# A two-layer graph attention and transformer block: work around the stage barrier and inside the attention slots moved

## What is computed

```python
def layer0(v, q, adj):            # v [8,512,512], q [8,512]; self features and masks
    self_feat = concat(v, q) @ W_self.T + b_self
    for d in range(2):            # two directions, 20 keys, 16 heads
        out += gat_attention(self_feat, ...)      # masked softmax over 20 keys
    return v + relu(out)

def layer1(hidden, w):            # hidden [8,512,512], 16 heads of 32
    h = sln(hidden, w)            # layer norm, scaled and shifted by rows from w
    q, k, v = split(h @ Wqkv.T + bqkv)
    att = softmax(q @ k.T) / sqrt(512)
    h1 = (att @ v) @ Wp.T + bp + hidden
    return sln(h1, w) + h1
```

## Time and profile before

| quantity | value |
|---|---|
| median of 3 runs | 1351.17 us (1349.26 to 1354.97) |
| profiled execution | 1355.45 us, its span 1353.6 us |
| TensorE busy | 1248.8 us (92%) |
| VectorE busy | 891.5 us (66%) |
| GpSimd busy | 882.3 us (65%) |
| ScalarE busy | 615.2 us (45%) |
| attention, first score matmul to last | 501.9 to 1323.8 us |
| VectorE maxima (L1635) | 496 of 674 ns |
| ScalarE exponentials (L1526) | 512 of 597 ns |
| GpSimd sums of 1024 columns (L1356, L1361) | 180 of 2.39 us |

### The profile page before, as it was taken

One profiled execution on the slowest core, in us unless ns is written; L12 is line 12 of the kernel. 1 busy time (PEld: TensorE's weight loads), 2 busy tenths in 40 slices (PEclk: granted clock), 3 DMA queues, 4 the chain that ended last, 5 costly groups with the idle time before them and its releaser, 6 DMA issues.

```text
span 1353.6 us, 20343 instructions
## 1 busy us (share of the span) xinstructions
PE 1248.8 (92%) x6100; PEld 831.7 (61%) x6100; DVE 891.5 (66%) x1448; ACT 615.2 (45%) x1076; POOL 882.3 (65%) x565
## 2 busy tenths in 40 slices
PE   7879899999999788899999999999999999999983
PEld 4347677777777666466656666666565566566551
DVE  3445578778778754756766776776675776676745
ACT  1322252445244434454454464464464455455452
POOL 1114467676776734765795796795796696696733
PEclk9979899999999888899999999999999999999987
DMA  9663254445444653433543442542442542542410
GB/s 340 253 224 110 63 191 172 157 158 222 159 155 146 202 192 89 126 86 72 149 110 71 135 124 67 142 123 65 139 127 56 144 116 69 145 116 69 115 47 32
DMA packets 104454, 178.60 MB, mean 132 GB/s; under 512 B 38832, under 2 KB 48368, under 8 KB 99104
## 3 DMA queue, kind: packets, MB, share of 16 engines
q1 hardware_dynamic: 92816, 145.22, 35.3%
q10 hardware_dynamic: 11536, 32.14, 7.9%
HBM read 81.04 MB, written 45.38 MB: 93 GB/s over the span
## 4 chain that ended last, share of the span: by engine, by line
PE 29%; DVE 12%; POOL 9%; issue 6%; DMA 3%; ACT 3%; SPq 1%; ACTq 0%; DVEq 0%; POOLq 0%
PE a_bank L1808 6%; PE a_bank L1759 6%; DVE rden L1653 5%; POOL acc L1361 4%; PE a_bank L1772 4%; PE a_bank L106 4%; DVE keep L1635 4%; PE a_bank L107 4%; PE a_bank L108 4%; PE a_bank L1819 2%; DMA out_y<-h 1%; ACT pt L1526 1%; POOL acc L1356 1%; DMA h<-h_rows 1%; DVE rden L1661 1%
## 5 line engine op out<-in xcount | busy, mean ns | idle before, releaser
L1635 DVE TENSOR_REDUCE keep<-a_bank 128x1 f32<-128x512 f32 x496 | 331.5, 674 | 256.5 <-PE a_bank L1772 254.1
L1526 ACT ACTIVATE pt<-a_bank 128x512 f32<-128x512 f32 x512 | 300.5, 597 | 376.5 <-PE a_bank L1759 322.9
L1361 POOL TENSOR_TENSOR acc<-acc,pt 128x1024 f32<-128x1024 f32 x120 | 286.5, 2387 | 32.4 <-ACT pt L1526 25.2
L1759 PE MATMUL a_bank<-sq_stack,sk_stack 98*128 98x512 f32 x512 | 221.7, 433 | 19.6 <-ACT pt L1526 7.5
L1772 PE MATMUL a_bank<-sk_stack,sq_stack 96*128 96x512 f32 x496 | 209.4, 422 | 4.5 <-DVE keep L1635 4.4
L1356 POOL TENSOR_TENSOR acc<-pt 128x1024 f32<-128x1024 f32 x60 | 143.6, 2393 | 77.4 <-PE a_bank L1819 65.4
L1759 PEld LDWEIGHTS a_bank<-sq_stack,sk_stack 98*128 98x128 f32 x512 | 98.0, 191 | 115.5 <-issue 71.7
L1065 PE MATMUL g_bank<-m,sf 128*128 128x320 f32 x512 | 147.5, 432 | 0.8 <-issue 0.8
L1653 DVE RECIPROCAL rden<-a_bank 128x128 f32<-128x128 f32 x128 | 120.6, 944 | 17.9 <-PE a_bank L1802 17.9
L1772 PEld LDWEIGHTS a_bank<-sk_stack,sq_stack 96*128 96x128 f32 x496 | 95.9, 193 | 48.6 <-DVE keep L1635 33.0
L1808 PE MATMUL a_bank<-pt,v 128*32 128x512 f32 x1024 | 124.7, 605 | 0.0
(11 more groups left out here) (200 smaller groups left out, 2496.0 us busy)
## 6 DMA issues: line engine op xcount, KB each, us to landing
sq_stack<-qh SPq DMA_DIRECT2D x256, 64.0 KB, 2.0
sk_stack<-kh SPq DMA_DIRECT2D x256, 64.0 KB, 2.1
m<-m_rows SPq DMA_DIRECT2D x8, 1280.0 KB, 6.7
xraw<-in_x_t SPq DMA_DIRECT2D x8, 1024.0 KB, 8.8
xn<-in_x SPq DMA_DIRECT2D x8, 1024.0 KB, 5.2
h_rows<-xn ACTq DMA_DIRECT2D x8, 1024.0 KB, 4.8
t_rows<-houth SPq DMA_DIRECT2D x8, 1024.0 KB, 3.9
t_rows<-houtl SPq DMA_DIRECT2D x8, 1024.0 KB, 6.5
```

The lines of the kernel that those rows point to most:

```text
L1361: nc.gpsimd.tensor_tensor(acc[:, two, :], acc[:, two, :], pt[:, step + 1, two, :], ALU.add).then_inc(s["sum_done"], 1)
L1526: nc.scalar.activation(pt[:, i, 2 * half + k, :], bank[:, k, :], ACT.Exp).then_inc(s["exp_done"], 1)
L1635: nc.vector.reduce_max(mx[:, half, k, n:n + 1], bank[:, 2 + e % 2, :], AX).then_inc(s["emax_done"], 1)
L1759: nc.tensor.matmul(bank[:, k, :], sk[c % 2][0:3 * DH + 2, j, i * P:(i + 1) * P], sq[c % 2][0:3 * DH + 2, j, :], start=True, stop=True).the ...
```

## The change

No computation is added or removed. In `graph`: in the last step GpSimd does its four scalings without `add_bp` between them and the four additions after them; VectorE scales a bias column later; SyncE issues the stacks of chunk 1, half 1, before the barrier and leaves the store of batch 7's rows to the next block. In `attention`: SyncE issues that store right behind the load of the output weights; the store of tile 0 stands between the copies of q and of k, those of tiles 2 and 3 and the row load come later. GpSimd does result 1 ahead of an `rsqrt`, result 2 at the start of chunk 3, result 3 at its end. ScalarE takes `project` of q in slot 3, the result copies in slot 10, `normalise` of tiles 2 and 3 later, `load_h` of tiles 0 and 1 in chunk 0 of the next batch and of tile 2 in slot 13, and the second part of `load_t` in slot 14. VectorE takes the low part of q in slot 3, the reciprocals in slots 4, 5, 7 and 8, the quotients in slot 9 and the low part of k in slot 10.

```diff
--- before.py
+++ after.py
@@ -467,7 +467,7 @@
         assert nc.sbuf_base == at["out"]
-        houth, houtl = sb("houth", [P, FC, N], F32R), sb("houtl", [P, FC, N], F32R)
+        houth, houtl = t["houth"], t["houtl"] = sb("houth", [P, FC, N], F32R), sb("houtl", [P, FC, N], F32R)
         assert nc.sbuf_base == at["acc"]
@@ -634,10 +634,11 @@
             stacks(1, 0)
+            stacks(1, 1)
             sp.wait_ge(la["sh_lo"], 1)
...
                          sht[:, 1, :].bitcast(F32)).then_inc(la["shrow_lo"], 16)
-            store_t(B - 1, 4 * B)
+            sp.wait_ge(s["hl_done"], 4 * B)
 
@@ -657,7 +658,7 @@
 
-            def softmax(b, has_former):
+            def softmax(b, has_former, last=False):
                 for i in range(NT + 2):
@@ -670,8 +671,11 @@
                         nc.gpsimd.tensor_tensor(v, v, keys(rc[:, i - 2]), ALU.mult).then_inc(s["w_done"], 1)
-                        if has_former:
+                        if has_former and not last:
                             add_bp(b - 1, i - 2)
+                if last:
+                    for i in range(NT):
+                        add_bp(b - 1, i)
 
@@ -707,7 +711,7 @@
                     lo_rows(b - 2)
-                softmax(b, True)
+                softmax(b, True, last)
 
@@ -1005,8 +1009,6 @@
 
-            dve.wait_ge(la["ld_c"], 16)
-            nc.vector.tensor_scalar(bcol3[:, 2, :], bcol3[:, 2, :], float(D) ** -0.5, None, ALU.mult).then_inc(la["bv_done"], 1)
             nonzero_rows(0)
@@ -1014,6 +1016,8 @@
             steps(dve, step)
+            dve.wait_ge(la["ld_c"], 16)
+            nc.vector.tensor_scalar(bcol3[:, 2, :], bcol3[:, 2, :], float(D) ** -0.5, None, ALU.mult).then_inc(la["bv_done"], 1)
             lo_part(0, 0)
@@ -1274,15 +1278,17 @@
         def _(sp):
-            def stacks(b, c, half):
+            def stacks(b, c, half, which=(0, 1)):
 
...
                     sp.wait_ge(s["et_ready"], SLOTS * (G - 2) + 8 * half + 8)
-                for ready, src, dst, at, done in (
-                        (s["qh_done"], qh, sq, (0, 2 * DH), stq), (s["ql_done"], ql, sq, (DH,), stq),
-                        (s["kh_done"], kh, sk, (0, DH), stk), (s["kl_done"], kl, sk, (2 * DH,), stk)):
+                for n, ready, src, dst, at, done in (
+                        (0, s["qh_done"], qh, sq, (0, 2 * DH), stq), (0, s["ql_done"], ql, sq, (DH,), stq),
+                        (1, s["kh_done"], kh, sk, (0, DH), stk), (1, s["kl_done"], kl, sk, (2 * DH,), stk)):
+                    if n not in which:
+                        continue
                     sp.wait_ge(ready, need)
@@ -1311,26 +1317,32 @@
                     later = not first(b)
-                    if c < 3 or more:
+                    if (c < 3 or more) and not start(b, c):
                         stacks(*ahead(b, c, 1), 1)
...
                     if c == 3 and later:
-                        store_y(b - 1, 3)
-                    if c == 3:
-                        load_rows(b)
+                        store_y(b - 1, 2)
+                    if c == 0 and not first(b) and not (isinstance(b, int) and b == 1):
+                        store_y(b - 2, 3)
+                    if c == 0 and later:
+                        load_rows(b - 1)
                     if c < 2 or more:
-                        stacks(*ahead(b, c, 2), 0)
+                        stacks(*ahead(b, c, 2), 0, (0,))
+                    if c == 1 and later:
+                        store_y(b - 1, 0)
+                    if c < 2 or more:
+                        stacks(*ahead(b, c, 2), 0, (1,))
                     if c < 3 or more:
                         shift_lo(*ahead(b, c, 1), 0)
-                    if c == 1 and later:
-                        store_y(b - 1, 0)
-                    if c == 2 and later:
-                        store_y(b - 1, 2)
 
             sp.dma_start(t["wp_raw"][:, :, :], d["wp_t"].rearrange("(c p) o -> p c o", p=P)).then_inc(w_in[3], 16)
+            for k, src in enumerate((t["houth"], t["houtl"])):
+                sp.dma_start(d["t_rows"][B - 1, k], src[:, :, :].bitcast(F32)).then_inc(t["t_stored"], 16)
             batches(sp, batch)
+            store_y(B - 2, 3)
+            load_rows(B - 1)
             for i, (y, _) in enumerate(last_tiles()):
@@ -1392,14 +1404,14 @@
                         key_sum(*(ahead(b, c, -1) if c else (b - 1, 3)), 1, 2)
+                    if later and c > 1:
+                        result(b - 1, c - 1)
                     if later and c in (1, 2):
                         rsqrt(b - 1, 2 * c - 2)
-                    if later and c in (2, 3):
-                        result(b - 1, 2 * c - 3)
                     if not final(b, c):
                         key_sum(b, c, 0, 0)
-                    if later and c in (1, 2):
-                        result(b - 1, 2 * c - 2)
+                    if later and c == 1:
+                        result(b - 1, 0)
                     if first(b) and c in (1, 2):
@@ -1421,6 +1433,8 @@
                         output_lo(b, 1)
+                    if later and c == 3:
+                        result(b - 1, 3)
 
@@ -1560,33 +1574,35 @@
                             values(b + 1, 1 - bpar, 0, KB)
-                        if slot == 2 and c in (2, 3) and later:
-                            normalise(b - 1, 2 * c - 3)
+                        if slot == 2 and c == 2 and later:
+                            normalise(b - 1, 1)
+                        if slot == 4 and c == 3 and later:
+                            normalise(b - 1, 3)
                         if slot == 2:
                             shift_hi(b, c, 1)
-                        if slot == 4 and (c < 2 or more):
+                        if slot == 3 and (c < 2 or more):
                             project(*ahead(b, c, 2), 0)
-                        if slot == 5 and c in (1, 2) and later:
+                        if slot == 4 + c and c in (1, 2) and later:
                             normalise(b - 1, 2 * c - 2)
...
                         if later:
-                            if slot == 15 and c == 1:
+                            if slot == 13 and c == 1:
                                 load_h(b - 1, 2)
...
                                 load_h(b - 1, 3)
-                        if slot == 1 and c == 3 and more:
-                            load_h(b, 0)
-                        if slot == 10 and c == 3 and more:
-                            load_h(b, 1)
+                        if slot == 6 and c == 0 and later:
+                            load_h(b - 1, 0)
+                        if slot == 8 and c == 0 and later:
+                            load_h(b - 1, 1)
                         if slot == 11:
...
                                 shift_hi(*ahead(b, c, 1), 0)
-                        if slot == 11 and c == 1 and more:
+                        if slot == 14 and c == 1 and more:
                             load_t(b + 1, (1,))
-                        if slot == 9:
+                        if slot == 10:
                             if c == 0 and later:
@@ -1703,17 +1719,17 @@
                                 variance(b - 1, 2 * c - 1)
-                        if slot == 5 and (c < 2 or more):
-                            lo_part(*ahead(b, c, 2), 0)
                         if slot == 3:
                             shift_lo(b, c, 1)
-                        if 4 <= slot < 8 and former:
-                            reciprocals(*former, slot - 4)
-                        if slot == 8 and former:
+                            if c < 2 or more:
+                                lo_part(*ahead(b, c, 2), 0)
+                        if slot in (4, 5, 7, 8) and former:
+                            reciprocals(*former, slot - 4 - slot // 6)
+                        if slot == 9 and former:
                             quotients(*former)
...
                             shift_lo(*ahead(b, c, 1), 0)
-                        if slot == 9 and (c < 2 or more):
+                        if slot == 10 and (c < 2 or more):
                             lo_part(*ahead(b, c, 2), 1)
```

## The result

The changed kernel takes 1336.15 us, the median of six runs (1324.51 to 1343.4), against 1353.3 for the kernel before on the same chips (1349.26 to 1357.35): a ratio of 0.986, with a 95% interval of 0.981 to 0.991. The change gains 17 us; 42 were forecast, and the time is 2 us above the upper end of the range. Its runs spread over 19 us, those of the kernel before over 8.

A forecast was written before the change was run, and what follows sets the result against it. TensorE was taken to bind, so only its gaps or slow matmuls could go. Gains of 30.3 + 6.5 + 2.3 + 2.0 - 2.4 + 3.6 = 42.3 us, off the median 1351.17, gave 1309 us; range 1297 to 1334.

The forecast's parts named there:

- stores and loads around chunk 1: Chunks 1 and 2: earlier store and load remove a 3.0 us loss, 1.2 left for late transfers; gain 1.8 a batch.
- graph's end: Before the barrier: four bias additions in a row on GpSimd end later, a loss of 2.4 us (1.5 to 3.5).
- the loop's edges: Batches 1 to 6: the window's 5 us beyond six times batch 3, of which half was kept.
- Spread reciprocals: VectorE, chunks 0 and 3: spreading its work stops TensorE's waits in slots 8 to 10; gain 1.2 us in both together.
- B: Rival: ScalarE's chain after the quotients binds, so spreading VectorE's work frees nothing; 1321 us, chance 0.13.
- GpSimd's results: Chunk 3, slot 3: reordered results bring chunk 2's last key sum earlier, so the denominators' stall goes; gain 1.6 us.
- the shift row: End of chunk 1: starts 0.6 us later, goes out 4 us ahead of use, needing as little as 3.67; fits narrowly.
- Rival A: Handover from chunk 1 to 2 becomes the new wait: 3.0 us instead of 1.2 in seven batches, 1322 us, chance 0.15.
- T: Experiments' rival theory, around chunk 1's end: DMA traffic is the limit, so any order of transfers leaves a wait somewhere.
- First chunk: Batch 0 after the barrier: stack copies issued before it remove ScalarE's 5.47 us wait; 23.2 us, 6.5 less.
- Rival E: Half 1's row lands after all moved stores, 6 us for 0.7, and splits hold GpSimd, 3 more: 1317 us, chance 0.04.
- Last batch: Chunks 0 and 1 gain 1.1 us, chunk 2 gains 3.5, chunk 3 loses 1.0 on result 2's low part; net 3.6.

The follow-up runs named there:

- e5: e2 with reciprocals back in slots 4 to 7, quotients in 8, low parts of q and k and ScalarE's copies as before: 1325.27 us, ratio 0.982.
- e6: e2 with the order of GpSimd's results and ScalarE's normalisation of tile 3 as in the kernel before: 1324.64 us, ratio 0.981.
- e2: Changed kernel with the load of tile 2's rows moved from slot 13 to 15, behind the second half in slot 14: 1312.53 us, ratio 0.971.
- e4: e2 with tile 0's store back behind the k copies and the shift row: 1323.41 us, ratio 0.980.
- e13: e1 with the load of tile 2's rows in slot 15 instead of 13: 1331.01 us, ratio 0.986.
- e14: e13 with tile 0's store back behind the k copies and the shift row: 1328.15 us, ratio 0.983.
- e9: e2 with the barrier as before: last rows' stores ahead of it, stack copies of chunk 1's second half behind it: 1315.61 us, ratio 0.976.
- e7: e2 with the bias additions of the graph's last batch back between GpSimd's scalings: 1313.29 us, ratio 0.972.
- e8: e2 with ScalarE's two copies of result 2 back in slot 9, in the last chunk only: 1314.14 us, ratio 0.972.
- e3: Kernel before with the second half of the next batch's rows in slot 14 of chunk 1 instead of 11: 1340.84 us, ratio 0.994.
- e1: Changed kernel with the second half of the next batch's rows back in slot 11 of chunk 1: 1329.09 us, ratio 0.985.
- e10: e1 with the second half moving a quarter of its columns, 256 KB instead of 1 MB, so computing something else: 1307.70 us, ratio 0.968.

## Why the prediction was wrong

The failed step is one term of the sum, the gain of 1.8 us a batch from the stores and loads around chunk 1; a smaller one, the graph's end, was off too and hidden by luck. All terms, against spans of the profiled executions:

| step | forecast | found |
|---|---|---|
| chunks 0 and 3, batches 1 to 6 | 16.8 | 18.2 |
| chunks 1 and 2, batches 1 to 6 | 10.8 (and 2.7 at the loop's edges) | -9.3 |
| batch 0 | 8.8 | 8.7 |
| graph's end and barrier | -0.4 | -2.3 |
| from the program's start to the graph's first bias addition, nothing changed | 0 | 2.1 |
| last batch up to its last slot | 3.6 | 0.6 |
| sum | 42.3 | 18.0 |

The 2.7 at the loop's edges weren't there: batch 3, from which the steady part was taken (102.0), was the second shortest of the six in the kernel before, whose mean is 102.9; most of the difference lies in chunk 1 of batch 2 (27.1) and chunk 3 of batch 4 (28.9).

- **Spread reciprocals.** Right: the earlier trace rows's surplus goes, slots 8 and 9 of chunk 0 take 1.16 to 1.18, and 0.2 to 0.3 a chunk is left behind ScalarE's result copies, of which I had left 0.3. e5 confirms it, and B was wrong.
- **GpSimd's results.** Right, 1.6 by e6; result 3 at the end of chunk 3 costs nothing.
- **Stores and loads around chunk 1.** The failed step. Its direction was named, "a wait of TensorE in slot 2 of chunk 2", and its arithmetic had the half 0.6 late. Two inputs were too small. The last issue was put 2.1 behind the start of slot 14 and came 2.9 behind it (849.14, slot 14 beginning at 846.23), because the load ahead of it waited for a store issued only 5.6 us earlier. And the landing was taken as the 5.8 of the earlier trace rows and was 7.4. The sum has the half at 856.5 instead of 854.1, against the 853.5 that I had as the need (TensorE was there at 853.7). From there on every us of lateness counts in full, so a surplus of 0.6 became 2.84; and I had booked no price for the slot behind a wait, in which the clock falls: 8.0 of the 30.4 us. The other half of the term, the shift row, was right: chunk 1 hands over without a wait in all six batches. The row goes out 3.5 to 3.8 us ahead of its use, as the narrow margin said, and completes in 2.5 to 3.5, since the second half now comes behind it; the 3.67 of the earlier trace rows was too much here.
- **Rival A** had the place and the sign, with 15% of the chances and a price of 3.0 a batch, copied from what the kernel before lost there. Nothing bounded it by that: the batch lost 5.1 there (30.4 in six). It should have been priced from the lateness, with "5.2 available, 5.8 needed" as the sign of a cliff, and its end put into the range.
- **What T adds.** Even a timely half is not free. It, its first half, the twelve copies and the store share the DMA engines, so in slot 11 it delays the k copies and the row, and in slot 14 it is itself late. I had treated the landing times as fixed and the edits as independent; e2, e4, e13 and e14 show that they are neither.
- **First chunk.** 23.05 against 23.2, in part by luck. The sum had 1.4 for the lower clock and 0.7 for the row; the row cost nothing and the lower clock 2.1 in slots 0 and 1, since slot 1 now ran at it throughout (2.19 us at a granted clock of 0.50, 1.65 at 0.70 before). Rival E had the order right and the price wrong: the stores were issued by 502.2 and the last took 10.2 us, to 511.9; the row, issued at 509.43, completed at 512.2, behind them, but slot 8 needs it only at 513.7. What the Trainium skill (DMA: Bandwidth & Descriptors, Queues, rings and completion order) says of ring order fits that row, without being shown by it.
- **Graph's end.** The wait is 2.9 us longer than in the kernel before and 3.3 longer than in e7, where I took 2.4 with an end of 3.5. The barrier opens 1.2 us sooner by e9 (41.5 us from ScalarE's copy to the first score matmul, 40.3 in e2), not 2.0. From the graph's first bias addition to the first score matmul the changed kernel takes 325.25 us and the kernel before 322.96. That attention began only 0.2 later was luck: the stretch ahead of that addition, the same code in both, took 176.91 instead of 178.96 (176.0 to 179.3 in the sixteen executions). Beside VectorE's weight splits three of the four additions take 1.71 and the first 1.27, and the four splits 6.75 together, 1.74 each, where one without an addition beside it takes 0.68 (e7). By the rule of the Trainium skill (SBUF — State Buffer, Who interferes with whom) each addition would have been held for a pass. The trace agrees that the two engines hold each other up, but not on the size: an addition beside a split loses 0.44, less than the 0.68 of a pass, and the first loses nothing.
- **Last batch.** Chunk 2 gained 3.1 (3.5 forecast). Chunk 3 lost 3.7 instead of 1.0: the low part was 1.56 later in slot 11, and the low clock behind the longer wait made slots 12 to 14 longer by 2.2. e8 takes both away (2.72, 0.93, 0.94 and 4.60).

Slots 0 to 3 of chunk 2 in e2 still take 0.6 us more a batch than without loss, and slot 15 ahead of them 0.9. The 0.9 is the wait for the row, which takes 3.9 to 5.8 us there; of the 0.6 most is batch 4, where slots 0 to 2 take 6.6 instead of 3.6 behind that wait. Why the row took 5.8 in batch 4 (slot 15 at 3.65) and 4.0 in batch 3 (1.76), issued 0.2 us behind the first load of the second half both times, stays open.

## What to carry to other kernels

When a load is moved behind an instruction that waits for another DMA, its time is that DMA's landing plus its own under the traffic of that moment; where the margin worked out so is below zero, price the whole lateness and the slow clock behind the wait, not a copy of an old stall. Where several edits touch transfers of one stretch, write one time table of issues and landings for it and move all of them together, because their prices don't add (11 us or nothing for the same store). Issue a small transfer that a matmul is about to need ahead of the megabytes. When one engine's issue of a load must wait, put it last among the issues of that engine, and look at what computation stands behind it.

## What the runs showed of the hardware

Small transfers on one queue were held up by large ones on another. SyncE's row of 4 KB at the end of chunk 1, from its issue to its last completion, batches 1 to 6:

| kernel | second half of the rows (ScalarE's queue), first load issued | row, us |
|---|---|---|
| changed | 1.5 to 2.5 us behind the row | 2.5 to 3.5 |
| e3 | 0.6 to 0.8 behind it | 2.5 to 3.8 |
| e2 | 0.0 to 0.3 ahead of it | 3.9 to 5.8 |
| before | 1.2 to 1.6 ahead | 5.1 to 6.9 |
| e1 | 1.8 to 3.5 ahead | 5.9 to 6.6 |
| e10, a quarter of the bytes | 2.1 to 2.5 ahead | 3.6 to 4.9 |

In batch 3 the k copies of 64 KB, issued on SyncE's queue, landed in 3.2 us in the changed kernel with only the store of 256 KB issued in the 4 us before, in 6.9 in e1 with 1 MB issued in the us before on ScalarE's queue, and in 4.1 in e10 with 256 KB there. The Trainium skill (DMA: Bandwidth & Descriptors, Queues, rings and completion order) says that both queues are rings on the same 16 DMA engines, and that a completion signal lands only after every earlier write of that engine, across its queues. The rows agree with it; I had drawn only on its sentence about one queue.

TensorE's clock fell from 2.4 to 1.2 GHz behind waits in slot 2 or slot 15 and came back within the next slots (0.69 is the mean over slot 3 of chunk 2, 0.50 the one behind the wait of the last chunk, where a matmul takes 0.63 us instead of 0.40). It didn't fall each time: in e13 a slot 15 of 3.47 us was followed by slots of 1.25 and 1.19, and one of 3.31 by 2.27 and 1.70.
